# Where the attention's output and the second norm are kept: one image pair's buffers, and when ScalarE fills the rows that are scattered

## The chip, the core and the metric

The kernel runs on one core of a Trainium2 chip. The core's engines are TensorE (PE in the profile, with its weight loads as PEld), VectorE (DVE), ScalarE (ACT), GpSimd (POOL) and SyncE (SP), which issues most of the transfers. The metric is the device time of one execution in microseconds, as a median over runs. Each engine runs its own list of instructions strictly in the order in which the program has them, and waits on semaphores that the other engines raise.

## The reference

Thirty-two images of 56x56 pixels with 64 channels pass through three layers. Each layer adds its result to its input.

```python
x = x + relu(conv3x3(group_norm(x), binarized_kernel))
t = x.reshape(32, 3136, 64)
t = t + attention(layer_norm(t))   # 8 heads, context = softmax(K) @ V, 1x1 products
t = t + moe(layer_norm(t))         # per token the best 2 of 8 experts
```

The expert layer takes the two best of eight gate logits for each token and adds `w * (gelu(xf @ W1[e] + b1[e]) @ W2[e] + b2[e])` for both. The gate reads the normalised token `xn`. The residual reads the token itself.

## The kernel before

**Pairs and turns.** The images go through the core in 16 pairs (`PAIRS`), and a pair has 2 x 3136 tokens. A buffer of one pair is `[128, 3136]`: 49 groups (`J`) of 64 channels, worked on in seven parts (`NB = 7`, index `b`) of 7 groups, so 448 columns each. One pass of the program is a turn. In turn `n` the convolution of pair `n` runs beside the attention, the norms, the gate and the routing of pair `n - 1` and the scatter of pair `n - 2`. There are 18 turns. The first five carry no expert work. From turn 5 on each turn also carries 12 expert blocks of 512 rows (`PER_TURN = 12`). Turns 6 to 14 are one hardware loop, and the others are written out. After the last turn 68 more blocks follow (`tail`), which contain expert work alone.

**What sets the order.** The table `STEPS` gives each step a slot per engine, between 0 and 366.1, with the distance from one part to the next and the number of turns by which the step lags (`1` in the third field). `program(engine)` sorts the steps and the block steps (`BLOCK_STEPS`, placed by `BLOCK_AT`) by slot. A slot is a place in the order, not a time. Nothing reorders at run time.

**The steps around the change**, for a pair, in order:

- `tok` (SP, slot 351.7): loads the pair's input into `x_tok` (1568 KB).
- `yt` (PE, then DVE): adds the convolution's result into `x_tok`. DVE does this at L1386. `yt` on DVE is the first step of a turn there.
- `ln_m` to `ln_c` with layer 0, `k`, `qv`, `exp`, `kt`, `cx`, `qn`, `qb`: the first norm and the attention. `keys` holds the keys and their exponentials and is last read by `kt`. `qn` is a division on POOL (L622), and PE's `qb` waits for it (L919).
- `out` (DVE, L1456): adds product, bias and `x_tok`, and writes the sum into `R`, columns 0 to 63. `R` is the buffer `[128, 49, 132]` whose 132-column rows are scattered to memory. It waits for the scatter of the same part of the previous pair.
- `ln_m` to `ln_c` with layer 1: the second norm. The centred value stands in `R`, columns 64 to 127 (`COL_X`), and `ln_c` writes the normalised value into `ln_x`, a buffer of two parts. So its part `b` waits for two readers of part `b - 2`.
- `xg` (PE L948, then ACT): PE transposes `ln_x`. ACT first copies `ln_x` into `R`'s columns 64 to 127 (L776, raising `xn_act`), then empties PE's bank into `xgT` (L784, L785). `lg` makes the gate's logits from it.
- `gate_a`, `route_a` (DVE), `rt` (two products on PE, L959), `gate_b`, `route_b` to `route_d` (DVE): weights and destinations. `gate_b` writes the two weights into `R` (L1253, L1255), and the first instructions of `route_b` read `rt`'s banks (L1259 after the first, L1263 after the second). `route_d` ends with `place_at` (L1285).
- `sc` (POOL, L640): 49 indirect transfers of `R`'s rows to their places, in the next turn.

**An expert block** `i`, in the order of its steps: `b_h0` (PE L978, then gelu on ACT L794), `b_ev` (ACT L800 takes block `i - 1`'s result out of its bank), `b_xt` (PE L996 turns block `i + 1`'s rows in, ACT L806 and L807 copy them to `xts`), `b_y0`, `b_h1` (L978 and L794 again), `b_yt` (PE L1004 turns block `i - 1`'s result back, DVE L1473, L1475 and L1479 combine it; L1004 also waits for `xts`), `b_y1` (PE L987, which waits for the second gelu), and the scatter of the result on POOL. Each `h` step on PE also waits until the gelu of the `h` step before it has read the bank.

At a turn's end the order on PE is, for blocks 10 and 11: L1004 (block 9's result), L987 (`b_y1` of 10), L978 (`b_h0` of 11), L959 (`rt` 0), L996, L959 (`rt` 1), L978 (`b_h1` of 11), L987, L1004, the first `yt`, L987.

Of the kernel before, what the change touches and what calls it, by code (L numbers as in the profile page):

```python
# [8 lines left out]
ALU = mybir.AluOpType  # L9
ACT = mybir.ActivationFunctionType  # L10
AX = mybir.AxisListType

IMAGES, HW, C = 32, 56, 64
# [52 lines left out]
for turn_ in range(FIRST_TURN, TURNS):  # L66
# [58 lines left out]
    ("xg", BATCHES, 1, dict(pe=(248.1, 2.95), act=(255.4, 1.94))),  # L125
    ("lg", BATCHES, 1, dict(pe=(253, 2.71), dve=(253.2, 2.07))),
# [68 lines left out]
def build_program(nc, x, conv, Wk, bk, Wq, bq, Wv, bv, Wr, br, Wg, bg, W1, b1, W2, b2, out):  # L195
    ctx = ExitStack()
    with ctx:  # L197
        def sb(name, shape, dt=F32):
            return ctx.enter_context(nc.sbuf_tensor(name, shape, dt))
# [24 lines left out]
        keys = sb("keys", [128, TOKENS])  # L224
        R = sb("R", [128, J, RW])
        ln_x = sb("ln_x", [128, 2, JB, C])
# [95 lines left out]
        def at(name, n, c):  # L322
            value = n * PER[name] + max(c, 0)
            return S[name], max(value, 0) if isinstance(value, int) else value
# [47 lines left out]
        def all_drained(n, *steps):  # L372
            return latest("pre_free", n, steps)
# [71 lines left out]
        def _(sp):  # L445
# [3 lines left out]
            def pre(n, name, *a):  # L449
# [15 lines left out]
                if name == "tok" and not (isinstance(n, int) and n == 0):  # L465
                    for free in all_drained(n, *((-1, ("out", b)) for b in range(NB - BANKS, NB))):
                        sp.wait_ge(*free)
                        sp.sem_inc(S["loading"], 1)
                    load_tok(n)
# [199 lines left out]
        def _(act):  # L669
# [28 lines left out]
            def pre(n, name, *a):  # L698
# [7 lines left out]
                if name == "ln_sq":  # L706
# [6 lines left out]
                    act.activation(ln_sq[:, :, :], xc[:, js, :] if layer == 0 else R[:, js, COL_X:COL_X + C], ACT.Square) \  # L713
# [55 lines left out]
                elif name == "exp":  # L769
                    act.wait_ge(*at("qs_dve", n, 2 * NB))  # L770
                    qt = QT[0:LC, :, :].rearrange("p h k -> p (h k)")
                    act.activation(qt, qt, ACT.Exp).then_inc(S["exp_act"], 1)
                elif name == "xg":
                    b = a[0]
                    act.wait_ge(*at("normed_dve", n, NB + b + 1))
                    act.copy(R[:, JB * b:JB * b + JB, COL_X:COL_X + C], ln_x[:, b % 2, :, :]) \  # L776
                        .then_inc(S["xn_act"], 1)
# [75 lines left out]
        def _(pe):  # L853
# [11 lines left out]
            def pre(n, name, *a):  # L865
# [76 lines left out]
                elif name == "xg":  # L942
                    b = a[0]
                    pe.wait_ge(*at("normed_dve", n, NB + b + 1))
                    xn = ln_x[:, b % 2, :, :].rearrange("p j c -> p (j c)")
# [143 lines left out]
        def _(dve):  # L1089
# [57 lines left out]
            def ln(n, name, layer, b=0):  # L1147
                k = layer * NB + b
                js = slice(JB * b, JB * b + JB)
                src = x_tok[:, js, :] if layer == 0 else R[:, js, 0:C]  # L1150
                centred = xc[:, js, :] if layer == 0 else R[:, js, COL_X:COL_X + C]
# [24 lines left out]
                else:  # L1176
                    if layer == 0:
                        normed = centred
                    else:
                        normed = ln_x[:, b % 2, :, :]  # L1180
                        if b < 2:
                            dve.wait_ge(*filled(n - 1, "xg", NB - 1))
                            dve.wait_ge(*at("xn_act", n, 0))
                        else:
                            dve.wait_ge(*filled(n, "xg", b - 2))
                            dve.wait_ge(*at("xn_act", n, b - 1))
                    dve.tensor_tensor(normed, centred, rstd[:, js].unsqueeze(2).to_broadcast([128, JB, C]), ALU.mult) \
                        .then_inc(S["normed_dve"], 1)

            def gate(n, name):  # L1190
# [54 lines left out]
                elif name == "gate_b":  # L1245
# [6 lines left out]
                    done(dve.tensor_tensor(g[:, 8, :], g[:, 7, :], g[:, 6, :], ALU.mult))  # L1252
                    done(dve.tensor_tensor(R[:, :, COL_W], g[:, 8, :], g[:, 5, :], ALU.max))  # L1253
# [75 lines left out]
            def pre(n, name, *a):  # L1329
# [57 lines left out]
                elif name == "k":  # L1387
                    b = a[0]
                    if b == 0 and isinstance(n, int) and n == 0:
                        dve.wait_ge(S["tables_stored"], 32)  # L1390
                    dve.wait_ge(*filled(n, name, b))
# [57 lines left out]
                elif name == "out":  # L1449
# [3 lines left out]

                    dve.wait_ge(*at(f"scattered{b}", n, 0))
                    js = slice(JB * b, JB * b + JB)
                    dve.scalar_tensor_tensor(R[:, js, 0:C], src, bkr[:, 1:2], x_tok[:, js, :], ALU.add, ALU.add) \  # L1456
# [81 lines left out]
```

## Time and profile before

| | |
|---|---|
| runs before | 3501.93, 3503.42, 3513.58 us, median 3503.42 |
| profiled execution, first to last instruction | 3490.5 us |
| median less that span | 12.9 us |
| busy time | PE 3003.7, DVE 2232.8, ACT 1883.4, POOL 1872.2 us |
| a turn without blocks | about 150.5 us (355.6 to 506.1) |
| a turn of the loop | about 191.2 us (1831.5 to 2022.7) |
| the blocks behind the last turn | from about 3090 us to the end |

The profiled execution's own time is not given beside its span, so 12.9 us is what lies between this span and the median of the runs. Busy time is the time in which an engine has an instruction under way. PE is busy for 86% of the span and is the fullest engine. In a turn of the loop PE is idle for 17 to 18 of 191 us. A row of a timeline gives the start, the duration, the instruction and, in brackets, how long the engine had been idle before it and what ended that.

### The profile page before, as it was taken

The numbers are of one execution on the slowest core, as the hardware profiler recorded it, in microseconds if no ns is written. First come the engines' busy times: TensorE is split into PE (matmuls) and PEld (weight loads), VectorE is DVE, ScalarE is ACT, GpSimd is POOL, SyncE is SP. The second block draws the span as 40 slices with busy tenths as digits, with TensorE's granted clock in tenths as the row PEclk, the third lists the DMA queues.
The fourth block names the chain that finished last, engine by engine and source line by source line (L and its number), as shares of the span: only waits on it lengthen the run. The fifth ranks groups of instructions, "written<-read, shape, count | busy, mean of one in ns | idle before, by whom it ended". The sixth has DMA issues, their size and how long they took to land. (4 is left out here: it accounts for less than half of the span.)

```text
span 3490.5 us, 60486 instructions
## 1 busy us (share of the span) xinstructions
PE 3003.7 (86%) x16878; PEld 1597.8 (46%) x16878; DVE 2232.8 (64%) x5060; ACT 1883.4 (54%) x3186; POOL 1872.2 (54%) x1837
## 2 busy tenths in 40 slices
PE   3787787989998988989998989899998977589997
PEld 2554555545554454544544444445454443123332
DVE  3677778686958576667768585867676767222222
ACT  2424243365655656565656555565656555357776
POOL 0006144264655647373746465564737374767777
PEclk6878787899999999999999999999999997799999
DMA  8304223142525242343425242424333221234442
GB/s 225 85 22 112 77 80 100 59 113 73 149 69 141 81 127 80 105 109 91 128 69 142 73 136 78 133 80 118 97 92 106 86 78 52 78 103 131 122 104 61
DMA packets 406813, 345.91 MB, mean 99 GB/s; under 512 B 258190, under 2 KB 347029, under 8 KB 400657
## 3 DMA queue, kind: packets, MB, share of 16 engines
q1 hardware_dynamic: 343632, 260.62, 28.4%
q0 software_dynamic: 53760, 78.84, 6.7%
q10 hardware_dynamic: 9088, 2.47, 0.4%
q8 instruction: 154, 2.52, 0.3%
q14 instruction: 179, 1.46, 0.1%
HBM read 261.66 MB, written 147.47 MB: 117 GB/s over the span
## 5 line engine op out<-in xcount | busy, mean ns | idle before, releaser
L640 POOL DMA_INDIRECT rows<-R,place_at x784 | 803.5, 1025 | 570.5 <-issue 513.3
L646 POOL DMA_INDIRECT out<-o_sb,xb x624 | 662.3, 1061 | 703.2 <-DVE o_sb L1479 413.2
L794 ACT ACTIVATE h_sb<-psum,w2b 128x512 f32<-128x512 f32 x624 | 393.6, 683 | 330.5 <-PE psum L978 326.6
L890 PE MATMUL psum<-xpad,conv_w 128*64 128x448 f32 x2688 | 538.3, 552 | 10.0 <-ACT xpad L723 7.5
L978 PE MATMUL psum<-xts,w1b 64*128 64x512 f32 x1248 | 389.1, 699 | 55.8 <-issue 29.3
L987 PE MATMUL psum<-h_sb,w2b 128*64 128x512 f32 x1248 | 352.0, 644 | 47.8 <-ACT h_sb L794 47.2
L890 PEld LDWEIGHTS psum<-xpad,conv_w 128*64 128x64 f32 x2688 | 188.5, 138 | 322.1 <-issue 309.5
L646 POOL DMA_INDIRECT out<-o_sb,xpad x272 | 272.3, 1001 | 107.9 <-issue 92.6
L757 ACT ACTIVATE conv_y<-psum 128x448 f32<-128x448 f32 x112 | 60.4, 540 | 358.2 <-PE psum L890 358.2
L913 PE MATMUL psum<-WT,conv_y 128*112 128x256 f32 x896 | 234.3, 394 | 12.7 <-DVE QT L1402 6.5
L622 POOL TENSOR_TENSOR QT<-QT,q_sum 112x512 f32<-112x512 f32 x112 | 120.4, 1081 | 229.4 <-DVE q_sum L1427 228.0
L748 ACT COPY xpad<-psum 128x448 f32<-128x448 f32 x224 | 142.5, 647 | 185.0 <-PE psum L877 182.0
L877 PE MATMUL psum<-ident,raw 112*128 112x112 f32 x896 | 148.2, 306 | 82.0 <-DMA raw<-in_x 30.7
L1491 DVE TENSOR_TENSOR y_w<-psum,xpad 128x512 f32<-128x512 f32 x68 | 47.0, 692 | 265.2 <-PE psum L1056 261.3
L824 ACT ACTIVATE h_sb<-psum,VT 128x512 f32<-128x512 f32 x272 | 172.0, 683 | 79.8 <-PE psum L1039 74.3
L900 PE MATMUL psum<-ident,conv_y 128*64 128x64 f32 x3136 | 199.2, 289 | 9.9 <-DVE x_tok L1386 9.1
L900 PEld LDWEIGHTS psum<-ident,conv_y 128*64 128x64 f32 x3136 | 185.8, 205 | 47.1 <-issue 30.4
L913 PEld LDWEIGHTS psum<-WT,conv_y 128*112 128x112 f32 x896 | 152.3, 180 | 111.0 <-issue 48.8
L978 PEld LDWEIGHTS psum<-xts,w1b 64*128 64x128 f32 x1248 | 104.0, 199 | 211.5 <-issue 161.6
L932 PE MATMUL psum<-KT,VT 112*128 112x128 f32 x896 | 136.6, 309 | 56.8 <-ACT KT L735 56.8
L877 PEld LDWEIGHTS psum<-ident,raw 112*128 112x128 f32 x896 | 109.5, 165 | 147.9 <-issue 81.7
L723 ACT ACTIVATE xpad<-xpad,gn 128x784 f32<-128x784 f32 (+2 forms) x160 | 160.0, 1034 | 30.8 <-DVE gn L1378 30.1
(230 smaller groups left out, 5546.0 us busy)
## 6 DMA issues: line engine op xcount, KB each, us to landing
rows<-rows SPq DMA_DIRECT2D x236, 264.0 KB, 6.0
xb<-rows SPq DMA_DIRECT2D x156, 264.0 KB
x_tok<-in_x SPq DMA_DIRECT2D x16, 1568.0 KB, 7.5
w2b<-w2x SPq DMA_DIRECT2D x312, 65.0 KB
w1b<-w1x SPq DMA_DIRECT2D x312, 64.2 KB
xpad<-rows SPq DMA_DIRECT2D x68, 264.0 KB, 2.7
raw<-in_x SPq DMA_DIRECT2D x32, 448.0 KB
raw<-in_x SPq DMA_DIRECT2D x32, 440.0 KB
```

Of the source, the lines that this page charges most:

```text
L640: pool.indirect_dma_start(rows[:, :], bass.IndirectOffsetOnAxis(ap=place_at[:, j:j + 1], axis=0), R[:, j, :], None) \
L646: pool.indirect_dma_start(out_rows, bass.IndirectOffsetOnAxis(ap=block_rows[:, t, COL_ID:COL_ID + 1].bitcast(U32), axis=0), tokens[:, t, : ...
L723: ins = act.activation(part, part, ACT.Identity, bias=shift[h, :], scale=scale[h, :])
L748: act.copy(dst, src[:, 0:448].rearrange("p (k r h) -> p r h k", k=4, h=2)) \
L794: act.activation(h_sb[:, e, q, :], psum[:, HB0 + e, :], ACT.Gelu, bias=w2b[:, i, e, 2 * C + q:2 * C + q + 1]).then_inc(S["h_ready"], 1)
L824: act.activation(h_sb[:, e, q, :], psum[:, HB0 + 2 * q + e, :], ACT.Gelu, bias=t_w2[:, k % TAIL_RING, e, 2 * C + q:2 * C + q + 1]).then_in ...
L877: ins = pe.transpose(dst[:, TQ * r:TQ * r + TQ], raw[0:TQ, 4 * grp + r, :], ident[0:TQ, 0:TQ])
L890: ins = pe.matmul(dst[64 * i:64 * i + 64, 0:BL], conv_w[:, t, :], xpad[:, i, r0:r0 + ROWS, dx:dx + HW], start=(t == 0), stop=(t == 5))
L900: ins = pe.matmul(dst[h, C * j:C * j + C], cols[:, JB * b + j, :], ident[:, h], start=True, stop=True)
L913: ins = pe.matmul(dst[0:LC, 256 * c:256 * c + 256], t[:, o:o + LC], WT4[:, 0:2, :].rearrange("p w m -> p (w m)"), start=True, stop=True)
L978: ins = pe.matmul(psum[:, HB0 + e, :], w1b[h, i, 128 * q:128 * q + 128], xts[h, i % 2, :], start=True, stop=True)
L987: ins = pe.matmul(psum[64 * e:64 * e + 64, YB, :], w2b[:, i, e, C * q:C * q + C], h_sb[:, e, q, :], start=(q == 0), stop=(q == 1))
```

## The change

`out` now adds into `x_tok` in place, without a wait for the scatter. The second norm reads `x_tok` and keeps centred and normalised values in the `keys` buffer (seen as `xn2`). `ln_c` normalises in place there. `ln_x` and the waits of `ln_c` for it are gone, and PE's `xg` reads `keys`. ACT's copy at `xg` is gone. A new step `rw` on ACT, slots 305 to 341, copies part `b` of `x_tok` into `R`'s columns 0 to 63 and part `b` of `keys` into columns 64 to 127, after it has waited for the scatter of the previous pair. Three waits move with it: `tok` on SP, which used to wait for the last `out` steps, waits for the last copy (`xn_act`); the first `k` of the next pair waits for the copies and the last `xg`; and `gate_b` waits for the scatters before it writes the weights into `R`.

```diff
     ("xg", BATCHES, 1, dict(pe=(248.1, 2.95), act=(255.4, 1.94))),
+    ("rw", BATCHES, 1, dict(act=(305, 6))),
     ("lg", BATCHES, 1, dict(pe=(253, 2.71), dve=(253.2, 2.07))),
...
+        xn2 = keys[:, :].rearrange("p (j c) -> p j c", c=C)
         R = sb("R", [128, J, RW])
-        ln_x = sb("ln_x", [128, 2, JB, C])
...
                 if name == "tok" and not (isinstance(n, int) and n == 0):
-                    for free in all_drained(n, *((-1, ("out", b)) for b in range(NB - BANKS, NB))):
-                        sp.wait_ge(*free)
-                        sp.sem_inc(S["loading"], 1)
+                    sp.wait_ge(*at("xn_act", n, 0))
+                    sp.sem_inc(S["loading"], 1)
                     load_tok(n)
...
+                elif name == "rw":
+                    b = a[0]
+                    js = slice(JB * b, JB * b + JB)
+                    act.wait_ge(*at("normed_dve", n, NB + b + 1))
+                    act.wait_ge(*at(f"scattered{b}", n, 0))
+                    act.copy(R[:, js, 0:C], x_tok[:, js, :])
+                    act.copy(R[:, js, COL_X:COL_X + C], xn2[:, js, :]).then_inc(S["xn_act"], 1)
                 elif name == "xg":
                     b = a[0]
-                    act.wait_ge(*at("normed_dve", n, NB + b + 1))
-                    act.copy(R[:, JB * b:JB * b + JB, COL_X:COL_X + C], ln_x[:, b % 2, :, :]) \
-                        .then_inc(S["xn_act"], 1)
...
-                    if layer == 0:
-                        normed = centred
-                    else:
-                        normed = ln_x[:, b % 2, :, :]
-                        if b < 2:
-                            dve.wait_ge(*filled(n - 1, "xg", NB - 1))
-                            dve.wait_ge(*at("xn_act", n, 0))
-                        else:
-                            dve.wait_ge(*filled(n, "xg", b - 2))
-                            dve.wait_ge(*at("xn_act", n, b - 1))
-                    dve.tensor_tensor(normed, centred, rstd[:, js].unsqueeze(2).to_broadcast([128, JB, C]), ALU.mult) \
+                    dve.tensor_tensor(centred, centred, rstd[:, js].unsqueeze(2).to_broadcast([128, JB, C]), ALU.mult) \
...
+                    all_scattered(dve, n)
                     done(dve.tensor_tensor(R[:, :, COL_W], g[:, 8, :], g[:, 5, :], ALU.max))
...
-
-                    dve.wait_ge(*at(f"scattered{b}", n, 0))
                     js = slice(JB * b, JB * b + JB)
-                    dve.scalar_tensor_tensor(R[:, js, 0:C], src, bkr[:, 1:2], x_tok[:, js, :], ALU.add, ALU.add) \
+                    dve.scalar_tensor_tensor(x_tok[:, js, :], src, bkr[:, 1:2], x_tok[:, js, :], ALU.add, ALU.add) \
```

Where the new step stands on ACT. This is the end of a turn with expert blocks as ACT has it before, from the convolution's last part (L757) to block 11's first gelu (L794). The names are those of the buffers: `y_sb` and `xts` belong to the blocks.

```order
L757 ACTIVATE conv_y<-psum 128x448
L800 ACTIVATE y_sb<-psum,w1b 128x512
L804 REGISTER_ALU
L806 COPY xts<-psum 64x512
L807 COPY xts<-psum 64x512
L791 REGISTER_ALU
L794 ACTIVATE h_sb<-psum,w2b 128x512 x2
L791 REGISTER_ALU
L794 ACTIVATE h_sb<-psum,w2b 128x512 x2
```

The same place with the change, its lines now four higher (L804 is the old L800, L810 and L811 the old L806 and L807). The brackets name the semaphores that an instruction waits for.

```order
L757 ACTIVATE conv_y<-psum 128x448 [waits pre_full2]
L777 REGISTER_ALU [waits normed_dve]
L778 COPY R<-x_tok 128x7x64 [waits scattered0]
L779 COPY R<-keys 128x7x64
L804 ACTIVATE y_sb<-psum,w1b 128x512 [waits yt_full,y_full]
L778 COPY R<-x_tok 128x7x64 [waits scattered1,normed_dve]
L779 COPY R<-keys 128x7x64
L778 COPY R<-x_tok 128x7x64 [waits scattered2,normed_dve]
L779 COPY R<-keys 128x7x64
L808 REGISTER_ALU
L810 COPY xts<-psum 64x512 [waits h_full,xt_full]
L811 COPY xts<-psum 64x512
```

One pair of copies now stands ahead of `b_ev`, and three ahead of the copies to `xts`. The continuation, up to block 11's first gelu:

```order
L778 COPY R<-x_tok 128x7x64 [waits scattered3,normed_dve]
L779 COPY R<-keys 128x7x64
L795 REGISTER_ALU
L798 ACTIVATE h_sb<-psum,w2b 128x512 [waits w_in4,y_full,h_full]
L798 ACTIVATE h_sb<-psum,w2b 128x512
L778 COPY R<-x_tok 128x7x64 [waits scattered4,normed_dve]
L779 COPY R<-keys 128x7x64
L778 COPY R<-x_tok 128x7x64 [waits scattered5,normed_dve]
L779 COPY R<-keys 128x7x64
L778 COPY R<-x_tok 128x7x64 [waits scattered6,normed_dve]
L779 COPY R<-keys 128x7x64
L795 REGISTER_ALU
```

Four pairs stand ahead of block 10's second gelu, and all seven ahead of block 11's first.

SP's order doesn't change, but what it waits for does. This is the load of `x_tok` in a turn without blocks, before and then with the change. `raw` is the next images' input, and L485 clears rows in memory.

```order
L494 DMA raw<-in_x 112x12x64 [waits pre_full2]
L495 DMA raw<-in_x 110x12x64
L485 DMA rows<-rows 16x4224 x9
L502 DMA x_tok<-in_x 128x3136 [waits pre_free3,pre_free1,pre_free0]
L485 DMA rows<-rows 16x4224
```

```order
L494 DMA raw<-in_x 112x12x64 [waits pre_full2]
L495 DMA raw<-in_x 110x12x64
L485 DMA rows<-rows 16x4224 x9
L502 DMA x_tok<-in_x 128x3136 [waits xn_act]
L485 DMA rows<-rows 16x4224
```

The load moved from behind the last `out` (slot 187 and on, on DVE) to behind the last `rw` (slot 341 on ACT), at the same place of SP's own list.

## Rows read from the trace of the kernel before

**Rows 1.** The page: span, and busy time of each engine

```profile
span 3490.5 us, 60486 instructions
...
PE 3003.7 (86%) x16878; PEld 1597.8 (46%) x16878; DVE 2232.8 (64%) x5060; ACT 1883.4 (54%) x3186; POOL 1872.2 (54%) x1837
```

**Rows 2.** Windows, PE: from:to, us, busy, granted clock, DMA share, GB/s

```profile
1831.50:2022.70 191.20, 173.81 (x1012) 0.94 0.38 104
1784.00:1805.00 21.00, 21.00 (x136) 1.00 0.21 61
1835.80:1842.00 6.20, 6.18 (x50) 0.50 0.41 147
```

**Rows 3.** Groups of PE's instructions, 1831.5 to 2022.7 us (one turn)

```profile
L978 PE MATMUL psum<-xts,w1b 64*128 64x512 f32 x96 | 30.2, 703 | 3.7 <-issue 3.3 <-ACT h_sb L794 0.4
L987 PE MATMUL psum<-h_sb,w2b 128*64 128x512 f32 x96 | 27.1, 644 | 3.9 <-ACT h_sb L794 3.8
...
L919 PE MATMUL psum<-ident,QT 112*128 112x112 f32 x28 | 4.4, 284 | 3.0 <-POOL QT L622 3.0
```

**Rows 4.** Timeline of ACT, 1789 to 1801 us: start, duration, instruction

```profile
1792.80 0.57 ACT L776 COPY R<-ln_x 128x448 f32<-128x448 f32 x1
1793.26 0.47 ACT L784 COPY xgT<-psum 128x384 f32<-128x384 f32 x1
```

**Rows 5.** Timeline of ACT, 1820 to 1831 us

```profile
1820.31 0.54 ACT L757 ACTIVATE conv_y<-psum 128x448 f32<-128x448 f32 x1 [2.77 <-PE psum L890]
1820.75 0.68 ACT L800 ACTIVATE y_sb<-psum,w1b 128x512 f32<-128x512 f32 x1
1821.45 0.58 ACT L806 COPY xts<-psum 64x512 f32<-64x512 f32 x1
1822.05 0.58 ACT L807 COPY xts<-psum 64x512 f32<-64x512 f32 x1
1822.65 1.26 ACT L794 ACTIVATE h_sb<-psum,w2b 128x512 f32<-128x512 f32 x2
1826.16 1.26 ACT L794 ACTIVATE h_sb<-psum,w2b 128x512 f32<-128x512 f32 x2 [2.24 <-PE psum L978]
```

**Rows 6.** Timeline of PE, 1820 to 1838.5 us

```profile
1822.85 0.66 PE L1004 MATMUL psum<-ident,y_sb 128*128 128x128 f32 x4
1823.97 1.08 PE L987 MATMUL psum<-h_sb,w2b 128*64 128x512 f32 x4 [0.47 <-ACT h_sb L794]
...
1826.75 0.30 PE L959 MATMUL psum<-cnt,before 128*128 128x28 f32 x2
...
1835.82 2.08 PE L978 MATMUL psum<-xts,w1b 64*128 64x512 f32 x4 [3.04 <-issue]
```

**Rows 7.** Timeline of DVE, 1820 to 1842 us

```profile
1823.54 0.69 DVE L1473 TENSOR_TENSOR y_w<-psum,xb 128x512 f32<-128x512 f32 x1 [2.84 <-PE psum L1004]
...
1827.78 0.18 DVE L1263 TENSOR_TENSOR cls<-cls,psum 128x28 f32<-128x28 f32 x1
...
1841.17 1.15 DVE L1386 TENSOR_TENSOR x_tok<-psum,x_tok 128x448 f32<-128x448 f32 x2 [2.75 <-issue]
```

**Rows 8.** Timeline of ACT, 1864 to 1866 us

```profile
1864.72 0.58 ACT L713 ACTIVATE ln_sq<-conv_y 128x448 f32<-128x448 f32 x1 [1.29 <-DVE lnv L1163]
```

**Rows 9.** Timeline of PE, 1866 to 1869 us

```profile
1866.50 1.97 PE L987 MATMUL psum<-h_sb,w2b 128*64 128x512 f32 x4 [2.88 <-ACT h_sb L794]
```

**Rows 10.** Timeline of DVE, 1848.9 to 1849 us

```profile
1848.94 0.19 DVE L1285 CAST place_at<-g 128x49 uint32<-128x49 f32 x1 [0.42 <-DVE g L1282]
```

**Rows 11.** Timeline of SP's queue, 1826 to 1832.5 us

```profile
1831.60 0.35 SPq L502 DMA_DIRECT2D x_tok<-in_x  x1
```

**Rows 12.** Timeline of ACT, 388 to 401 us

```profile
392.56 0.54 ACT L757 ACTIVATE conv_y<-psum 128x448 f32<-128x448 f32 x1 [3.54 <-PE psum L890]
```

**Rows 13.** Timeline of DVE, 403 to 408 us

```profile
405.81 1.16 DVE L1386 TENSOR_TENSOR x_tok<-psum,x_tok 128x448 f32<-128x448 f32 x2
```

**Rows 14.** DMA issues, 355 to 363 us: count, KB, us to landing

```profile
x_tok<-in_x SPq DMA_DIRECT2D x1, 1568.0 KB, 6.5
```

More of the change, by code:

```diff
@@ L712, in pre @@
                     js = slice(JB * b, JB * b + JB)
-                    act.activation(ln_sq[:, :, :], xc[:, js, :] if layer == 0 else R[:, js, COL_X:COL_X + C], ACT.Square) \
+                    act.activation(ln_sq[:, :, :], (xc if layer == 0 else xn2)[:, js, :], ACT.Square) \
                         .then_inc(S["ln_act"], 1)
@@ L944, in pre @@
                     pe.wait_ge(*at("normed_dve", n, NB + b + 1))
-                    xn = ln_x[:, b % 2, :, :].rearrange("p j c -> p (j c)")
+                    xn = keys[:, BL * b:BL * b + BL]
                     for m in range(4):
@@ L1149, in ln @@
                 js = slice(JB * b, JB * b + JB)
-                src = x_tok[:, js, :] if layer == 0 else R[:, js, 0:C]
-                centred = xc[:, js, :] if layer == 0 else R[:, js, COL_X:COL_X + C]
+                src = x_tok[:, js, :]
+                centred = (xc if layer == 0 else xn2)[:, js, :]
                 sums, var, rstd, t = (lnv[:, layer, i, :] for i in range(4))
@@ L1390, in pre @@
                         dve.wait_ge(S["tables_stored"], 32)
+                    if b == 0:
+                        dve.wait_ge(*filled(n - 1, "xg", NB - 1))
+                        dve.wait_ge(*at("xn_act", n, 0))
                     dve.wait_ge(*filled(n, name, b))
```

## The prediction, made before the changed kernel ran

> **What bounds the kernel now.** I read the page first. PE is busy for 3003.7 of 3490.5 us, the fullest engine [rows 1], so what matters is what makes PE stand still. The windows then say where: a turn of the loop lasts 191.2 us with PE busy for 173.8 us of it, at a mean granted clock of 0.94 [rows 2]. Its idle 17.4 us are not spread out. By the groups of PE's instructions in that turn, 3.3 us lie before one L978 (the engine waits for nothing: the loop's branch), 3.8 us before L987 for a gelu, and 3.0 us before L919 for POOL's division [rows 3]. Two of these are due to DVE. ACT sits 1.29 us before a norm's square and waits for DVE [rows 8]; the gelu behind that square lets PE's L987 start 2.88 us late [rows 9]. POOL divides between the scatters that it could begin when DVE had written `place_at`. So a turn has a ring: DVE's routing, DVE's first steps of the next turn, POOL, PE, and back to the routing through `rt`. A delay put on the last part of that ring comes back in full every turn. A delay of PE alone, up to about 2.9 us, would vanish in the L987 wait.
>
> **What the change takes away.** Seven copies of 0.57 us (L776) leave ACT in the stretch where PE transposes for the gate [rows 4], and DVE's waits for them go. Who waited there on the path? PE is busy for 21.00 of the 21 us of that stretch, at full clock [rows 2]. It fills the banks in its own order, and `lg` and the gate behind it come when PE comes. I cost the gain at nothing. What hides it is PE's own work; without that cover it would be at most 7 x 0.46 = 3.2 us a turn. The scatter wait of `out` also goes. PE is as full in the stretch of `out` as behind it, so I count nothing for that wait either.
>
> **What it adds: the price of a pair of copies.** One old copy starts and the next instruction starts 0.46 us later [rows 4]. L806 and L807 start 0.60 us apart [rows 5]. So two copies take 0.92 to 1.20 us. They are the same operation as L776, and the first of each pair has two waits, as L806 has, which starts 0.02 us after its forerunner's end instead of before it. I take 0.46 + 0.54 = 1.0 us, with 0.92 and 1.16 as ends. The Trainium skill ("ScalarE: Activation LUTs", What ACT_TABLE_LOAD costs) gives 186 ns + 0.833 ns per column without pointer operands, with back-to-back instructions overlapping by 93 ns. That would be 559 ns and 0.93 us per pair, which is the low end; by it the sum below would be 5 us smaller. The trace agrees on the single copy, 0.57 us.
>
> **Where the copies push (a turn with blocks).** ACT takes the convolution's part at 1820.31. Before, L800, L806, L807 and the gelu follow at once; the next gelu comes after 2.24 us of idling [rows 5]. Now:
> - One pair stands ahead of L800 and two more ahead of L806, so `xts` is ready at 1820.75 + 0.7 + 1.2 + 3 x 1.0 = 1825.65 instead of 1822.63. PE's L1004 starts 2.85 us later than its 1822.85 [rows 6]. DVE's combine waits for it already (2.84 us at 1823.54) [rows 7] and starts as much later. Behind it on DVE stands `gate_b`.
> - Four pairs stand ahead of block 10's second gelu. It ends at 1823.9 + 4.0 = 1827.9. PE's L987 waits for it and moves from 1823.97 to 1827.95, so by 4.0 us. Behind it on PE stand L978, both `rt` products and L996. The second `rt` ended at 1827.05 [rows 6] and now ends at 1831.0.
> - DVE's reader of it started at 1827.78, 0.7 us after it was ready [rows 7]. It now starts at 1831.1. DVE is 3.3 us late, and from there it works without a pause up to the next turn's first `yt` at 1841.17.
> - The other three pairs use up the 2.24 us and delay block 11's first gelu to about 1832.3. PE is then some 5 us late, but that excess over DVE's 3.3 us vanishes in the 2.88 us wait [rows 9].
>
> **The clock.** PE now stands still for 2.85 us ahead of L1004 and for 1.6 us ahead of L987 (1827.95 less the end of L1004, 1826.35). After the loop's gap of 3.04 us four L978 took 2.08 us [rows 6], and the granted clock was 0.50 for the next 6.2 us [rows 2]. After the 2.88 us gap L987 took 1.97 us instead of 1.08 [rows 9, 6]. So each gap of about 3 us in this trace is followed by the lower level, 1.2 GHz. I expect it here too. From L987 to the second `rt` lie 3.08 us of work at full clock. At 1.8 times (1.97 / 1.08) that is 2.3 to 2.5 us more. Then DVE is 3.3 + 2.3 = 5.6 us late per turn.
>
> **The sum.** Copies beside blocks occur in turns 5 to 15, eleven times: 11 x 5.6 = 61.6 us. Turn 16 has the copies too, but no convolution and more idle time: I take 2 us, between 0 and 5.6.
>
> In turns without blocks ACT is idle when the copies come. They start at 393.0 (end of L757 [rows 12]) and end at 400.0. Only then does SP issue the load of `x_tok`, which took 6.5 us to land [rows 14], so 406.6. DVE's first `yt` started at 405.81 [rows 13]: 0.8 us late, four times (pairs 1 to 4), 3 us. In the loop the load was issued at 1831.60 [rows 11], behind the last copy's end (about 1831.2) with no loss, and DVE comes for it 3 to 6 us later than before, so it costs nothing there. SP queues only clears and `raw` loads behind it, and those wait for later things.
>
> `gate_b`'s seven waits cost about 0.4 us of DVE, as the seven ahead of `place_at` do [rows 10], but it would then wait for `rt` anyway. `out`, `ln_m`, `ln_x` and `ln_c` do the same work on other buffers: nothing. The wait of the first `k` is long fulfilled.
>
> Total 61.6 + 2 + 3 = 67 us. The profiled span 3490.5 becomes 3557; the median lies 12.9 us above that span, so **3570 us**. With both ends of the copies' price and with the lower clock it is 11 x 5.3 + 1 = 59 up to 11 x 6.3 + 8 + 5 = 82 us, so 3562 to 3586.
>
> **Rivals.**
> - *The delay is right, the clock stays up.* 11 x 3.3 + 1 + 3 = 40 us: 3544 us (with the copies' ends 3537 to 3556). For it: the two gaps are interrupted by L1004, and whether the lower level comes depends on more than one gap. Against it: together they are 4.5 us of 6.
> - *No change.* PE's order lets the delay vanish, for instance because DVE has slack that I don't see between the routing and `place_at`. Against it: the only long pause of DVE from there to the first `yt` is the loop's branch, 2.75 us [rows 7], which moves along. It gives 3503 us, plus or minus 10.
> - *Faster.* The seven copies that leave the gate's stretch let `lg` finish earlier, by up to 3.2 us in 16 turns: 3503 - 51 = 3452 us. It decides only if PE has idle time in that stretch, more than the 3.3 us added behind it. PE has none there in a loop turn [rows 2].
> - *Still slower: the load of `x_tok` comes late.* If the last copy ends more than 3 us after 1831.6, `yt` waits in every turn. Another 3 us a turn give 3603 us.
>
> **How the numbers follow.** The forecast with the lower clock has 0.50, the clock staying up 0.28, no change 0.09, faster 0.07, the late load 0.06. Range: from 3530 us, below the second case's lower end, to 3588 us, above the first case's upper end; about 0.2 is left out. The likeliest case alone is 3562 to 3586. A measurement here can tell about 0.3% (10 us). Faster by more than that 0.07, within it 0.08, slower 0.85.
>
> **What would show it.** In the profile after: two copies at 0.46 us from start to start; the idle time of PE before the last-but-one L1004 and L987 of a turn up by 2.9 and 1.1 us; L978 and L987 behind them at about 2 us per four; a loop turn of 196 to 197 us instead of 191.2 (194.5 if the clock stays up); no new idle time of DVE before the first `yt` in the loop; about 151.3 us for a turn without blocks. I am wrong if a loop turn is still 191 us, if PE's idle time before L919 or the norm-bound L987 falls by as much as is added, or if the blocks' gelus don't move.

## The result, and the profile after

The changed kernel takes 3592.62 us (median of four runs, 3583.06 to 3596.07), the kernel before 3505.4 us in the same call. The ratio is 1.0238, 95% interval 1.0209 to 1.0267. So it is slower by 2.4%, and 22.6 us slower than predicted. The page of its profiled execution, beside [rows 1]:

```profile
span 3580.7 us, 60545 instructions
...
PE 3044.6 (85%) x16878; PEld 1625.4 (45%) x16878; DVE 2225.0 (62%) x5060; ACT 1936.6 (54%) x3298; POOL 1872.8 (52%) x1837
```

PE has the same 16878 products and is busy for 40.9 us longer. Most of that is the clock. By the clock's records PE works for 508 us at the lower level, 446 before, and half of the difference, an estimate of 31 us, is time added by it. The other 49.3 us of the span's growth is idle time. Where did the growth of 90.2 us arise? I compared the starts of each turn's first `yt` on DVE. In turns 1 to 4 the difference grows to 3.8 us. Turn 5, the first with blocks, takes 199.74 us instead of 180.19, so 19.6 us more. Turns 6 to 15 take 65.3 us more together, and everything from turn 16 on another 1.5.

**The end of a turn.** ACT and PE of the changed kernel at the place of [rows 5] and [rows 6], in one turn of the loop:

```profile
1272.76 0.54 ACT L757 ACTIVATE conv_y<-psum 128x448 f32<-128x448 f32 x1 [2.77 <-PE psum L894]
1273.20 0.56 ACT L778 COPY R<-x_tok 128x448 f32<-128x448 f32 x1
1273.65 0.57 ACT L779 COPY R<-keys 128x448 f32<-128x448 f32 x1
1274.12 0.69 ACT L804 ACTIVATE y_sb<-psum,w1b 128x512 f32<-128x512 f32 x1
...
1278.93 1.26 ACT L798 ACTIVATE h_sb<-psum,w2b 128x512 f32<-128x512 f32 x2
```

```profile
1274.95 1.08 PE L991 MATMUL psum<-h_sb,w2b 128*64 128x512 f32 x4 [0.59 <-ACT y_sb L804]
1277.90 1.10 PE L1008 MATMUL psum<-ident,y_sb 128*128 128x128 f32 x4 [1.87 <-ACT xts L811]
1280.25 1.97 PE L991 MATMUL psum<-h_sb,w2b 128*64 128x512 f32 x4 [1.24 <-ACT h_sb L798]
1282.15 2.08 PE L982 MATMUL psum<-xts,w1b 64*128 64x512 f32 x4
...
1285.15 0.30 PE L963 MATMUL psum<-cnt,before 128*128 128x28 f32 x2
...
1292.82 1.13 PE L982 MATMUL psum<-xts,w1b 64*128 64x512 f32 x4 [1.91 <-issue]
```

And DVE, at the place of [rows 7]:

```profile
1279.05 0.69 DVE L1469 TENSOR_TENSOR y_w<-psum,xb 128x512 f32<-128x512 f32 x1 [6.00 <-PE psum L1008]
...
1285.49 0.18 DVE L1258 TENSOR_TENSOR cls<-cls,psum 128x28 f32<-128x28 f32 x1 [0.31 <-PE psum L963]
...
1299.06 1.16 DVE L1381 TENSOR_TENSOR x_tok<-psum,x_tok 128x448 f32<-128x448 f32 x2 [3.14 <-issue]
```

Count from L757, which starts at 1820.31 before and at 1272.76 here. The last-but-one L1008 (L1004 before) starts 5.14 us behind it instead of 2.54, so 2.6 later. L991 starts 7.49 instead of 3.66 behind, so 3.8 later, and it and the next L982 take 1.97 and 2.08 us: the lower level. The second `rt` ends 12.69 instead of 6.74 us behind. DVE reads it 5.3 us later and starts `yt` 5.4 us later. All of this is the push that the prediction described. The idle times in it are smaller than predicted, 1.87 us ahead of L1008 and 1.24 ahead of L991 instead of 2.85 and 1.6.

**The turn as a whole.** The windows of three loop turns, and of 20 us from the gate's first transposes (L952) in two of them:

```profile
1104.60:1299.10 194.50, 172.09 (x1018) 0.96 0.36 102
2094.90:2288.90 194.00, 170.68 (x1000) 0.96 0.37 103
1891.50:2094.90 203.40, 182.38 (x1037) 0.91 0.35 98
```

```profile
2030.10:2050.10 20.00, 20.00 (x105) 0.73 0.18 49
2232.40:2252.40 20.00, 20.00 (x132) 1.00 0.17 49
```

The turn of 194 us is only 3 us longer than one of before [rows 2], although DVE is pushed by 5.4: in it L757 comes 168.1 us after the turn's first `yt`, and 170.5 before. Its PE is idle longer but busy for about 2 us less, at 0.96 instead of 0.94. The place is some 100 us into the turn, where PE waits twice for POOL's division. The kernel before and then the changed one:

```profile
1749.00:1757.00 8.00, 6.88 (x21) 0.57 0.09 27
```

```profile
1204.00:1212.00 8.00, 6.30 (x32) 1.00 0.13 34
```

Before, the two waits take 1.86 and 1.12 us and the clock falls. Here they take 1.03 and 1.70 us and it stays up.

Then there are turns of 197 to 203 us. Five of the ten turns 6 to 15 are such. What they take beyond 194.1 us each adds up to 27 of the 65.3 us. The other 38 us are what ten turns of 194.1 us take more than the ten of before, whose mean is 190.3 us. The PE of the longer turns shows no new gap. They differ in the gate's stretch: PE is busy throughout in both windows, but the granted clock is 0.73 in one and 1.00 in the other.

**Turn 5.** SP's queue and PE at its start:

```profile
704.38 0.35 SPq L502 DMA_DIRECT2D x_tok<-in_x  x1
706.09 0.38 SPq L508 DMA_DIRECT2D xb<-rows  x1
```

```profile
711.61 1.12 PE L1000 MATMUL psum<-ident,xb 128*128 128x128 f32 x4 [11.13 <-DMA xb<-rows]
```

The kernel before, in SP's queue:

```profile
656.63 0.36 SPq L502 DMA_DIRECT2D x_tok<-in_x  x1
658.34 0.38 SPq L508 DMA_DIRECT2D xb<-rows  x1
```

The first block's rows (`xb`) are loaded behind `x_tok`. That load now waits for the last copy, which ends at 704.29. PE stands for 11.1 us for rows that used to be on their way 48 us earlier. The first transposes of the gate come 140.7 us after the turn's first `yt`, 132.1 before, and the clock falls in the stretch behind them too: it is 0.75 there, 1.00 before.

### The profile page after: what moved, and what is told of

It reads as the page before. It is cut to its first block and busy times, and to the rows that moved or that the text cites. A ratio compares the mean times of both kernels' runs of the same rounds, so it can differ in the third digit from the quotient of the medians.

```text
span 3580.7 us, 60545 instructions
## 1 busy us (share of the span) xinstructions
PE 3044.6 (85%) x16878; PEld 1625.4 (45%) x16878; DVE 2225.0 (62%) x5060; ACT 1936.6 (54%) x3298; POOL 1872.8 (52%) x1837
## 5 line engine op out<-in xcount | busy, mean ns | idle before, releaser
L982 PE MATMUL psum<-xts,w1b 64*128 64x512 f32 x1248 | 389.5, 698 | 47.6 <-ACT h_sb L798 28.0
L991 PE MATMUL psum<-h_sb,w2b 128*64 128x512 f32 x1248 | 364.7, 664 | 66.8 <-ACT h_sb L798 59.7
L757 ACT ACTIVATE conv_y<-psum 128x448 f32<-128x448 f32 x112 | 60.4, 540 | 358.0 <-PE psum L894 358.0
L982 PEld LDWEIGHTS psum<-xts,w1b 64*128 64x128 f32 x1248 | 104.4, 198 | 206.1 <-issue 154.3
L1458 DVE TENSOR_TENSOR QT<-psum,bg_sb 128x56 f32<-128x56 f32 x112 | 24.3, 217 | 251.9 <-PE psum L959 251.8
```

The source lines that it names most:

```text
L982: ins = pe.matmul(psum[:, HB0 + e, :], w1b[h, i, 128 * q:128 * q + 128], xts[h, i % 2, :], start=True, stop=True)
L991: ins = pe.matmul(psum[64 * e:64 * e + 64, YB, :], w2b[:, i, e, C * q:C * q + C], h_sb[:, e, q, :], start=(q == 0), stop=(q == 1))
```

## The experiments

All times below are medians, and ratios are to the kernel before in the same call. The times of turns and clocks are those of one profiled execution of each. "Gate's clock" is the granted clock of the 20 us that start with the gate's first transposes, in the eleven turns 6 to 16. It was 1.00 in 8 turns of the kernel before and 0.74, 0.83 and 0.91 in the others. In the changed kernel it was 1.00 in four, 0.83 in four and 0.73 to 0.74 in three.

**1. First blocks' loads ahead of x_tok's** (`begin()` holds them).

```diff
                 if name == "tok" and not (isinstance(n, int) and n == 0):
                     sp.wait_ge(*at("xn_act", n, 0))
                     sp.sem_inc(S["loading"], 1)
+                    if isinstance(n, int) and n == FIRST_TURN - 1:
+                        begin()
                     load_tok(n)
```

> The changed kernel with one thing moved: in turn 4, SP issues the first expert blocks' three loads ahead of the load of x_tok instead of behind it. Theory 1 (of the 19.5 us that the turn before the first block turn grew by, some 14 are those loads, held up behind an x_tok load that now waits for the last copy): PE's 11.1 us idle before the first block's transposes goes to near 0, the turn shrinks from 199.7 to 185-189 us, and the run takes 3578-3584 us, 9 to 14 less than the changed kernel's 3592.6. Rival (the first blocks are late for something else, for instance POOL's scatters): the gap stays and the time is 3590-3596.

Measured: 3581.55 us, ratio 1.0205 (1.0174 to 1.0236), 11 us less than the changed kernel's median. Turn 5 takes 186.1 us instead of 199.7. The first block's rows came early, and no wait is left before their transposes:

```profile
644.16 0.37 SPq L510 DMA_DIRECT2D xb<-rows  x1
...
706.11 0.35 SPq L504 DMA_DIRECT2D x_tok<-in_x  x1
```

Theory 1 holds. Of the 13.6 us, 8.4 lie ahead of the gate's first transposes, where the rows were missing. The other 5.2 lie behind them, where the gate's clock is 1.00 here and was 0.75. Whether the queue brought that fall too isn't shown. The times alone wouldn't carry the reading, as the two intervals overlap: the profiled span is 3582.6 us, no shorter than the changed kernel's, because its turns 6 to 15 happened to take 12 us more, with the gate's clock below 1.00 in nine of the eleven turns. PE's vanished wait carries it, though behind those transposes PE now stands 4.6 us before the first product, 1.3 in the changed kernel.

**2. Copies of one element.**

```diff
-                    act.copy(R[:, js, 0:C], x_tok[:, js, :])
-                    act.copy(R[:, js, COL_X:COL_X + C], xn2[:, js, :]).then_inc(S["xn_act"], 1)
+                    act.copy(R[0:1, js.start, 0:1], x_tok[0:1, js.start, 0:1])
+                    act.copy(R[0:1, js.start, COL_X:COL_X + 1], xn2[0:1, js.start, 0:1]).then_inc(S["xn_act"], 1)
```

`R` is set to zero at the start, so the experts get zeros instead of tokens. Whether the zeros by themselves change the time wasn't tested.

> The changed kernel with each of the 14 copies of a turn cut to a single element, at the same place and with the same waits; R is set to zero once at the start, so that the rows go out with zeros where the tokens were (their weights, destinations and the blocks' counts are as before, the values are left out). Theory 1 (ACT's time in the copies is what delays PE and DVE in the loop): a copy of one element should take some 0.1-0.2 us, so 14 of them 1.5-2.5 us instead of 6.5; ring delay of the third pair at most 0.9 us. Loop turn 191.5-193 us, run 3515-3535 (of it 3-14 us from the late x_tok load of turns 1 to 4 and what stands behind it on SP). Rival 1 (the new waits or the new buffers cost the time, not the copies): loop turn stays at 194-200 us and the run above 3570. Rival 2 (the copies cost, but nothing is left of the SP part either): 3503-3512.

Measured: 3530.45 us, ratio 1.0058 (1.003 to 1.0086). ACT's groups in one loop turn:

```profile
L779 ACT COPY R<-keys 1x1 f32<-1x1 f32 x7 | 1.3, 186 | 0.0
L778 ACT COPY R<-x_tok 1x1 f32<-1x1 f32 x7 | 1.3, 181 | 0.0
```

Most of the loss goes with the copies' length. The waits and the order are untouched, so they are not the main cost. The rest is more than the turns of about 192 us that I expected: the loop's take 189 to 199 us, and the gate's clock is below 1.00 in eight of eleven.

**3. The copies alone, in the kernel before.** Neither in-place norm nor moved waits.

```diff
+    ("rw", BATCHES, 1, dict(act=(305, 6))),
...
+                elif name == "rw":
+                    b = a[0]
+                    js = slice(JB * b, JB * b + JB)
+                    act.wait_ge(*at("normed_dve", n, NB + b + 1))
+                    act.copy(keys[:, BL * b:BL * b + BL].rearrange("p (j c) -> p j c", c=C), R[:, js, 0:C])
+                    act.copy(VT[:, :, :].rearrange("p h k -> p (h k)")[:, BL * b:BL * b + BL].rearrange("p (j c) -> p j c", c=C), R[:, js, COL_X:COL_X + C])
```

> The kernel before with 14 extra copies of 448 columns per turn on ACT in the same slots 305 to 341, from R into buffers that are free there (nobody reads them); all else as before, the seven old copies too. Theory 1 (place and length of the copies make the loss in the loop, not the moved data): loop turns of 194 to 203 us as in the changed kernel, so before + 65 us in turns 6 to 16, with neither the step of turn 4 (SP's x_tok load still waits for out) nor the four short turns' loss: 3562-3575 us. Rival (the gain from taking seven copies out of the gate's stretch and the wait of out hides part of a bigger loss): more than 3580. Rival 2 (buffers and waits matter): below 3540.

Measured: 3587.71 us (3557.74 to 3604.13), ratio 1.0252 (1.0217 to 1.0288). That is some 13 us above theory 1's range and inside the rival's (over 3580), although turn 5 takes 187 us here. So it stays open whether the copies that leave the gate's stretch hide part of a bigger loss. The profiled execution was the fastest of them, and its turns 6 to 13 take 194.0 to 201.8 us, as in the changed kernel. Fourteen late copies alone are enough for the loop's loss. The spread of 46 us in one kernel is a sign of the other part. Two gate's stretches of this one execution, with the same instructions in the same order:

```profile
2015.90:2035.90 20.00, 20.00 (x132) 1.00 0.17 48
2209.20:2229.20 20.00, 20.00 (x106) 0.73 0.18 48
```

**4. Copies early**, behind each part's `xg`, where the old ones stood: slots `act=(255.5, 1.94)`.

> The changed kernel with the new step's slots moved from 305-341 to 255.5-267, right behind each xg part, where the seven old copies stood; data flow and waits unchanged. There ACT has seven copies more than before. Theory 1 (only the place costs): loop turn 191-191.6 us, x_tok load early again, 3498-3512 us, no different from the kernel before. Rival 1 (the in-place norm, keys as buffer, gate_b's waits cost something by themselves): 3515-3540. Rival 2 (14 copies instead of 7 in the gate's stretch hold up xgT and lg): PE idle in that stretch, up to 7 x 0.46 = 3.2 us a turn, 3530-3555.

Measured: 3543.67 us, ratio 1.0097 (1.0065 to 1.0129). It fits rival 2's time but not its mechanism: PE shows no idle time there. The gate's clock is between 0.72 and 0.78 in ten of eleven turns. One turn and its gate's stretch:

```profile
1485.80:1683.50 197.70, 179.82 (x1006) 0.91 0.37 101
1625.30:1645.30 20.00, 20.00 (x110) 0.78 0.19 49
```

The fourth and fifth group of 16-column products take 1.16 and 1.11 us, just ahead of the fall, where the kernel before has 1.06: PE seems held up by tenths that do not count as idle. Seven more copies in this stretch do cost, through the clock, though seven fewer were worth nothing.

**5. Half the copies late**: the normalised part's at `xg`, `x_tok`'s in slots 305 to 341.

> The changed kernel with the normalised part's copy back at xg (seven copies of 0.57 us in the gate's stretch, as before), and only x_tok's copy left in slots 305 to 341: seven late copies instead of fourteen. Theory 1 (the delay goes by the copies that stand ahead of the second rt: two ahead of block 10's second gelu by 2 x 0.5 us less...): four pairs pushed it by some 3.3 us, four single copies push it by 4 x 0.47 = 1.9 us; a loop turn where the clock in the gate's stretch stays up takes 192.5-193 us (194.1 in the changed kernel), and the run is 15 to 20 us shorter than the changed kernel without the clock's part: 3565-3580. Rival 1 (the low clock in the gate's stretch comes by where a turn falls, not by how late it is): some turns at 193, others at 198-200, run anywhere in 3550-3590. Rival 2 (it is the position of the copies ahead of xts, not their number): no less than 3588.

Measured: 3571.69 us, ratio 1.0151 (1.012 to 1.0183). The time lies in theory 1's range, but the turns follow rival 1:

```profile
895.60:1086.30 190.70, 168.99 (x1003) 0.96 0.39 106
2072.80:2274.30 201.50, 179.12 (x1018) 0.92 0.36 99
```

Where the gate's clock is 1.00 a turn takes 190.6, 191.1 or 193.4 us, against 188.5 to 191.6 before. In eight turns it is 0.67 to 0.76, and the loop's six among them take 198.5 to 201.5.

**6. Copies between gate and routing**, slots `act=(275, 2.5)`, with run 1's edit.

> The changed kernel with the copies' slots at 275 to 290 (seven pairs between the gate's stretch and the routing, where ACT stood idle for 3.4, 4.5 and 2.8 us), and the first blocks' loads ahead of turn 4's x_tok load. Theory 1 (late place costs through rt; gate's stretch is PE's): no gap on the ring is touched, loop turn 191 us or less, 3495-3512 us. Rival 1 (the clock in the gate's stretch goes low by where the turn falls): turns of 191 with 7 to 17 us at the lower clock near offset 147, 3530-3560. Rival 2 (the copies now hold up the gate's exp or the convolution's part): new DVE idle before the step behind the exp, 3515-3530.

Measured: 3561.65 us, ratio 1.0129 (1.0098 to 1.016). Theory 1 fails for this place, and the time is just above rival 1's range. The loop's turns with the gate's clock at 1.00 take 191.5 to 197.3 us, so the clock there isn't all. Three pairs stand ahead of a gelu there, as in slots 305 on, and PE waits for it:

```profile
2434.38 0.65 PE L1010 MATMUL psum<-ident,y_sb 128*128 128x128 f32 x4 [0.69 <-ACT xts L813]
2436.73 1.98 PE L993 MATMUL psum<-h_sb,w2b 128*64 128x512 f32 x4 [1.69 <-ACT h_sb L800]
```

**7. A delay of DVE alone**, in the kernel before, behind the reader of the second `rt`.

```diff
                         .then_inc(pre_free(n, ("rt", 1)), 1)
+                    dve.memset(keys[:, :], 0.0)
                     dve.wait_ge(*emptied(n, "rt", 0))
```

> The kernel before with one VectorE memset of 3136 columns (some 2.7 us by the row of 3584 columns in 3.045 us) behind the reader of the second rt, into the keys' buffer, which nobody reads then. ACT, its copies and all buffers as before. Theory 1 (from rt to the next turn's place_at the ring has no slack, so VectorE's delay comes back in full): loop turn 191.2 + 2.7 = 193.9 us, 11 turns, 30 us, and with some turns at a lower clock in the gate's stretch as in the changed kernel (each 3 to 9 us more) 3535-3580 in all. Rival 1 (delay alone, clock as before): 3535-3542. Rival 2 (VectorE has slack, the copies' loss in the changed kernel came through PE alone): 3503-3515.

Measured: 3562.36 us (3545.92 to 3577.53), ratio 1.0133 (1.0083 to 1.0182). The memset takes 2.7 us. The ring is real, but not rigid: loop turns with the gate's clock at 1.00 take 194 and 192 us in turn, and three with 0.73 to 0.77 take 198 to 202. In turns 1 to 4 it costs 3.0 to 3.3 us each.

**8. A part of the convolution in the middle of the gate's products**: `cv` at `pe=(154.3, 25.5), act=(160, 25.1)` instead of `pe=(152.3, 23.91), act=(158.1, 23.4)`.

> The changed kernel with the convolution's steps at PE slots 154.3 + 25.5 b instead of 152.3 + 23.91 b: on PE one part of the convolution (24 products of 448 columns) now stands in the middle of the gate's transposes and 16-column products instead of ahead of them. Instructions and data as in the changed kernel. Theory 1 (the lower clock at offset 147 comes from the row of short products there, and costs 3 to 9 us in about half of the turns): no turn has low clock in that stretch any more, all loop turns 193.5-195 us, run 3592 - 25 to 35 = 3555-3570. Rival 1 (the low clock there is set by the gap at the turn's end and by when the turn starts): turns of 197 to 203 us as before, 3580-3600. Rival 2 (the convolution's later parts make PE or the norm late): 3595 or more.

Measured: 3635.91 us, ratio 1.0329 (1.0296 to 1.0363). By the 20 us window the gate's clock is 0.88 to 1.00 in ten of eleven turns, against 0.73 to 1.00. But the 24 products put in push the rest of the row back by 4.7 us, and the fall goes with it, out of the window. The window and what follows, in turn 7:

```profile
1269.60:1289.60 20.00, 19.66 (x120) 0.90 0.13 33
1285.00:1299.00 14.00, 14.00 (x46) 0.52 0.26 69
```

In the 31 us from the gate's first transposes the lower level appears in eight of eleven turns, in the changed kernel in seven. Theory 1 fails: longer products in the middle don't keep this stretch at full clock. The order also costs otherwise. Turns 1 to 4 take 155 to 157 us instead of 150 to 152, and PE waits longer for gelus in the loop.

**9. Copies in ACT's idle times**, with run 1's edit.

```diff
-    ("rw", BATCHES, 1, dict(act=(305, 6))),
+    ("rw", BATCHES[0:4], 1, dict(act=(274.85, 0.06))),
+    ("rw", BATCHES[4:6], 1, dict(act=(297.2, 0.5))),
+    ("rw", BATCHES[6:7], 1, dict(act=(335, 6))),
```

> The changed kernel with the first blocks' loads ahead of turn 4's x_tok load and the seven pairs of copies put where ACT stood idle before: four pairs behind the result of the block ahead of the convolution's part 5 (4.5 us idle), two behind the gelu that follows the gate's exp (2.8 us), one in the 2.2 us ahead of block 11's first gelu. Theory 1 (a copy on ACT costs only if a gelu or xts stands behind it with PE waiting): PE waits as in the kernel before, a turn without low clock in the gate's stretch takes 190-191.5 us, and the run is 3490-3515 if the stretch stays at full clock in most turns. Rival 1 (by where turns fall against the clock's changes): the same base, but several turns of 197-200 us with 7 to 17 us of low clock near offset 147, run 3515-3545. Rival 2 (the in-place norm in the keys' buffer or gate_b's waits cost by themselves): base turn above 193 us, 3530-3560.

Measured: 3519.9 us (twelve runs), ratio 1.0036 (1.0013 to 1.0059). PE's waits in a loop turn are those of [rows 3] again:

```profile
L986 PE MATMUL psum<-xts,w1b 64*128 64x512 f32 x96 | 30.1, 702 | 4.0 <-issue 3.5 <-ACT h_sb L802 0.4
L995 PE MATMUL psum<-h_sb,w2b 128*64 128x512 f32 x96 | 27.2, 647 | 3.9 <-ACT h_sb L802 3.8
```

Most turns take 189 to 191.3 us, two with a gate's clock of 0.73 take 197.7 and 195.5. The copies' place decides most of it. The median lies in rival 1's range, 5 us above theory 1's, and the profiled execution (3508.07 us) is one of the quicker ones.

**10. The pair taken apart**: `x_tok`'s copy behind its norm's square (`act=(205.3, 3.81)`), the normalised part's at `xg`, run 1's edit.

> The changed kernel with the first blocks' loads ahead of turn 4's x_tok load and the pair of copies taken apart: x_tok's part is copied right behind its norm's square (slots 205.3 on, where out's writing into R was), the normalised part at xg where the seven old copies stood. ACT has seven more copies per turn than before, none of them late and none in the gate's stretch. Theory 1 (place alone): base turn 191 us as before, 3495-3515. Rival 1 (ACT is short of time there too, and out's squares and the blocks' gelus come late): new PE waits for gelus near offsets 110 to 140, base turn 192-195, 3515-3550. Rival 2 (the data flow costs by itself): base turn above 193 with no new wait for ACT.

Measured: 3510.19 us (twelve runs), ratio 1.0004 (0.9985 to 1.0024). No change can be measured in the whole. The in-place buffers, `gate_b`'s waits and the 14 copies are all in it. Its parts are not all alike, though. In the profile turns 1 to 4 take 592.7 us, 601.5 before. Turns 5 to 15 take 2109.0 us, against 2083.3 and 2094.1 in two executions of the kernel before (the second is run 11), and the gate's clock is below 1.00 in eight of eleven turns instead of three. So what these parts cost and gain is about even, not shown to be nothing each.

**11. The delay of run 7 in turn 5 alone**, as it was meant.

```diff
                         .then_inc(pre_free(n, ("rt", 1)), 1)
+                    if isinstance(n, int) and n == FIRST_TURN:
+                        dve.memset(keys[:, :], 0.0)
                     dve.wait_ge(*emptied(n, "rt", 0))
```

> The kernel before with VectorE's memset of 3136 columns in turn 5 alone (once, 2.7 us); the nine turns of the loop and all others are the code of before. Theory 1 (whether the gate's stretch falls to the lower clock depends on when it comes, so one delay can cost later turns time): at least one loop turn with low clock near offset 147 and 194-199 us long, until the turns fall as before again; run 3508-3530, that is more than the 2.7 us added. Rival (the clock answers to what PE does in the turn itself): all loop turns 190.5-191.6 us, run 3505-3512 (before plus at most 2.7).

Measured: 3506.5 us, ratio 1.0006 (0.9976 to 1.0036). The delay isn't in the program. Here `n` is the number of the pair, and pair 5 is routed in turn 6, which belongs to the hardware loop, where `n` is no Python integer. So the condition never holds. The trace has no memset of `keys` (run 7's has 16) and 60486 instructions, as before. This is the kernel before once more, and it decides nothing about theory 1. It does show how far two executions of one program differ: turn 15 takes 194.0 us here with a gate's clock of 0.72, and 186.0 us with 1.00 in the other profile. The turns of the loop take 188.6 to 193.8 us here and 188.5 to 193.8 in the other.

**12. Split, and the gate's stretch freed**: run 10 with the normalised part's seven copies moved to slots `act=(274.85, 0.03)`.

> The split kernel (x_tok's part copied behind its norm's square, first blocks' loads ahead of turn 4's x_tok load), with the normalised part's seven copies taken out of the gate's stretch too: they stand in the 4.5 us in which ACT was idle ahead of the convolution's part 5 (7 x 0.46 = 3.2 us). No copy is in the gate's stretch and none is late, the change's only possible gain without its price. Theory 1 (PE sets the gate's stretch, so taking copies out of it is worth nothing; a copy costs only where PE waits behind it): base turn 190.5-191.5 us, run within 0.3% of the kernel before, 3497-3517, and not better than the split kernel. Rival 1 (freeing ACT in the gate's stretch lets lg and the gate finish sooner): base turn 188-190, 3460-3495. Rival 2 (more turns with a low clock near offset 147): 3518-3540.

Measured: 3518.58 us (twelve runs), ratio 1.0018 (1.0001 to 1.0036). That is 1.6 us above theory 1's range, at the lower edge of rival 2's. Its loop turns take 191.5 to 193.6 us, and one 198.2, and the gate's clock is below 1.00 in seven of eleven turns. Freeing ACT beside the gate's products brings nothing. No run here is faster than the kernel before.

## Why the prediction was wrong

- **What bounds, and the gain at nothing: right as far as shown.** PE sets the pace. Run 12 takes the seven copies out of the gate's stretch without the late ones and gains nothing. Run 3, which keeps them there and has the late ones too, is slower than expected and leaves room for a small gain.
- **The price of a pair: right, at its low end.** In turn 4 fourteen copies start 0.47 us apart (below), so 0.93 us a pair where I took 1.0. An estimate from the figures of the Trainium skill ("ScalarE: Activation LUTs", What ACT_TABLE_LOAD costs) is 0.93 too, and its fixed part of 186 ns is what run 2's copies of one element take. The two waits of a pair did not break the overlap.

```profile
697.68 0.56 ACT L778 COPY R<-x_tok 128x448 f32<-128x448 f32 x1
698.13 0.57 ACT L779 COPY R<-keys 128x448 f32<-128x448 f32 x1
...
703.73 0.56 ACT L779 COPY R<-keys 128x448 f32<-128x448 f32 x1
```

- **The push at the turn's end: right.** Predicted 2.85 us for L1004, 4.0 for L987 and 5.6 for DVE with the clock; measured 2.6, 3.8 and 5.3. The lower clock behind the gaps came too, although they were shorter than predicted.
- **5.6 us a turn comes back in full: wrong in its parts.** The sum 61.6 us for turns 5 to 15 stands against 65.3 for turns 6 to 15 and 5.9 left of turn 5 in run 1, so 9.6 us more. That it comes so near is in part luck, for two errors offset each other. A turn with a quiet gate's stretch is only 3 to 4 us longer, because PE ran at 0.96 instead of 0.94 and took part of the push back. I had no term for that. The other 27 us come from a place that I costed at nothing, the gate's stretch. It was at full clock in the one turn whose rows I read [rows 2], and was not in three of the eleven turns of the same trace.
- **The failed step: "SP queues only clears and `raw` loads behind it".** True in the loop, false in turn 4, where `begin()` has its fifteen loads behind `x_tok`'s. PE waits 11.1 us for them, and the sum had no term for it. With these loads ahead (run 1) the median falls by 11 us, to 3581.55 us, inside the range that was given. Turn 5 gets 13.6 us shorter, of which 5.2 stand where the gate's clock differs. The 13.6 and the 9.6 us above make 23.2, against the 22.6 us missed; the terms left over are small and of both signs.
- **Turns without blocks: right.** Predicted 0.8 us each and 3 in all, measured 3.8 in all:

```profile
407.06 1.15 DVE L1381 TENSOR_TENSOR x_tok<-psum,x_tok 128x448 f32<-128x448 f32 x2 [1.84 <-DMA x_tok<-in_x]
```

- **Turn 16: right**, 1.5 us for 2. **From span to median:** I added the 12.9 us between one profiled span and a median. The profiled execution before was a quick one: in every run here the time is only 2 to 4 us above its own span. The changed kernel's profiled execution was a quick one as well, 11.9 us below the median, so the 12.9 fitted by luck. Span against span the change costs 90.2 us, median against median 87.2.
- **The rivals.** No change and faster did not come. "The clock stays up" is right about a quiet turn's length (194.5) for the wrong reason: the clock did fall at the gaps. The late load of `x_tok` happened outside the loop alone.

**What stays open.** Shown is that the gate's stretch runs at either level with the same instructions back to back (run 3), that this costs some 3 to 9 us a turn, and that with seven more copies beside it the clock falls in nearly every turn (run 4). Longer products between don't prevent the fall (run 8). Why it falls in one turn and not in the next is open. The place in the turn alone doesn't decide: in run 3 the stretch begins 137.2 to 137.4 us after the first `yt` in seven of the turns 6 to 14, and its clock is 1.00 in two of them and 0.73 to 0.83 in five. That the moment at which it comes decides was only argued, and no run here tests it. The Trainium skill ("TensorE: Matmul & The Clock Gate", A second HAM failure mode: psum-queue depth-cycling) tells of short idle times between groups of matmuls, from cycling through PSUM banks, that make the clock swing. No row here shows such idle times inside a busy stretch; the longer groups of run 4 are the nearest to it.

## What to carry to other kernels

When an edit delays a wait at the head of a DMA queue, look at what stands behind it in every turn, the written-out first and last ones above all, not only in the loop. Work on an engine with spare time is free only where no result that the full engine waits for stands behind it: the same 14 copies cost 2% at one place (run 1) and nothing that can be measured at another (run 10). And where the fullest engine's clock moves, read every turn's clock before costing a stretch at nothing, and follow the stretch itself, not a window of fixed length, when its order changes. Before a run is read, look for the instruction that it adds in its trace.

## What the runs showed of the hardware that I had not expected

The granted clock can fall in a stretch that counts as fully busy: 0.73 in 20 us of mostly transposes and 16-column products without a gap. Two executions of one program can differ in it, by 8 us in one turn (run 11). Less idle time is no sure gain, and more no sure loss: the 190.7 us turn of run 5 has PE busy for 169.0 us and idle for 21.7, the 191.2 us turn of the kernel before 173.8 and 17.4 [rows 2].
